# Reordering the first third of a cross-attention and MoE kernel on four engine queues

## The reference: what is computed

```python
def fake_quant(x, scale, zp):
    q = jnp.clip(jnp.round(x / s + z), 0, 255)
    return (q - z) * s
x = x + tanh(g_xattn) * (fake_quant(layernorm(x)) @ fake_quant(ctx))
# then, on layernorm(x): a router (softmax, 2 of 16 experts), the chosen experts and a shared one
z = silu(xt @ sw1 + sb1) * (xt @ sw2 + sb2) @ sw3 + sb3
x = x + tanh(g_ffn) * (y + z)
```

## Time and profile before

| | us |
|---|---|
| median of 3 runs (326.96 to 329.57) | 327.06 |
| the profiled execution's own time | 326.59 |
| its span, first to last instruction | 324.7 |
| PE busy | 299.0 |
| DVE busy | 186.0 |
| ACT busy | 104.7 |
| POOL busy | 25.7 |

### The profile page before, as it was taken

One profiled execution on the slowest core, in us unless ns is written; L12 is line 12 of the kernel. 1 busy time (PEld: TensorE's weight loads), 2 busy tenths in 40 slices (PEclk: granted clock), 3 DMA queues, 4 the chain that ended last, 5 costly groups with the idle time before them and its releaser, 6 DMA issues.

```text
span 324.7 us, 4586 instructions
## 1 busy us (share of the span) xinstructions
PE 299.0 (92%) x1892; PEld 151.5 (47%) x1892; DVE 186.0 (57%) x330; ACT 104.7 (32%) x113; POOL 25.7 (8%) x33
## 2 busy tenths in 40 slices
PE   0369879989999999999999999999999999999995
PEld 0234379964444444644444444444444344444442
DVE  2876897785698863585362565378674542110111
ACT  2888266868682450110343301313111000000000
POOL 2100120110000310000000011110121100000000
PEclk9999999999999999999999999999999999999999
DMA  7999044239960455000697600000000011300111
GB/s 285 415 314 290 1 131 131 63 96 230 308 215 0 91 105 129 2 2 0 182 342 256 219 40 2 0 0 0 2 0 0 4 67 67 129 28 36 67 65 65
DMA packets 34163, 35.55 MB, mean 109 GB/s; under 512 B 16068, under 2 KB 28380, under 8 KB 34012
## 3 DMA queue, kind: packets, MB, share of 16 engines
q1 hardware_dynamic: 34128, 35.23, 34.6%
...
HBM read 27.88 MB, written 4.20 MB: 99 GB/s over the span
## 4 chain that ended last, share of the span: by engine, by line
PE 80%; DVE 8%; SPq 7%; ACT 1%; DMA 1%; issue 1%; POOL 1%; DVEq 0%
PE PS L1312 26%; PE PS L1155 19%; PE PS L1369 19%; PE PS L1190 6%; PE PS L1102 6%; SPq L256 4%; DVE stats L662 2%; DVE areaW L716 2%; PE PS L1109 1%; DMA sbr<-in_L_ffn_sb_dram 1%; SPq L248 1%; DVE X L733 1%; PE PS L1171 1%; DVE wrow L742 1%; PE PS L1197 1%
## 5 line engine op out<-in xcount | busy, mean ns | idle before, releaser
L1155 PE MATMUL PS<-areaT,areaW 128*128 128x512 f16 x288 | 62.6, 379 | 1.4 <-DVE SA L747 1.4
L1155 PEld LDWEIGHTS PS<-areaT,areaW 128*128 128x128 f16 x288 | 28.0, 98 | 34.8 <-DVE SA L747 1.6
L1312 PE MATMUL PS<-areaT,area 128*128 128x512 f16 x192 | 41.6, 379 | 0.0
L1312 PE MATMUL PS<-areaT,areaW 128*128 128x512 f16 x192 | 41.6, 379 | 0.0
L896 DVE SCALAR_TENSOR_TENSOR X<-PS,cf,X 128x512 f32<-128x512 f32 x16 | 12.0, 751 | 47.6 <-PE PS L1369 47.1
L1102 PE MATMUL PS<-area,areaQ 128*128 128x512 f16 x128 | 30.5, 389 | 0.9 <-DVE area L699 0.5
L1312 PEld LDWEIGHTS PS<-areaT,area 128*128 128x128 f16 x192 | 18.8, 98 | 22.7
L1312 PEld LDWEIGHTS PS<-areaT,areaW 128*128 128x128 f16 x192 | 18.8, 98 | 22.7
L662 DVE BATCH_NORM_STATS2 stats<-X 128x6 f32<-128x512 f32 x32 | 20.5, 682 | 4.4 <-DMA X<-in_x_dram 4.2
L1369 PE MATMUL PS<-SW,areaH 128*128 128x512 f16 x96 | 22.0, 379 | 0.0
L1369 PE MATMUL PS<-areaW,QI 128*128 128x512 f16 x96 | 22.0, 379 | 0.0
...
## 6 DMA issues: line engine op xcount, KB each, us to landing
...
```

The costliest lines, as they stand in the source:

```text
L1155: last = mm(PS[:, SU_BANK[half * SC + c] + w, lo:hi], SW[:, wp, 2 * c + w, k, :], XT[:, xp, k, tk], start=(k == 0 and n == 0), stop=(k == ...
L1312: last = mm(PS[:, EU_BANK[u] + w, :], W12S[j][:, wp, k, cs], XT[:, xp, k, b * S:(b + 1) * S], start=(k == 0 and n == 0), stop=(k == KC - 1 ...
```

## The change

It touches order alone, on SP, ACT, DVE and PE, with one more small root on POOL. No matmul is added or taken away.

- **SP** interleaves the loads: tile 0, chunk 0, tile 1, chunks 1 to 4, tile 2, chunks 5 and 6, tile 3, chunk 7. The two bias loads into `sbr` stand ahead of the four weight chunks instead of behind them.
- **POOL** takes the roots of tiles 2 and 3 one by one, so that the counts on `coef1` become 1 to 6 instead of 1 to 5.
- **ACT** quantizes chunk 0 first and chunks 2 to 5 before tile 2; it copies all four turned tiles itself (before, DVE copied tiles 2 and 3); `ln_rows` writes the f16 rows first and the f32 rows second, for all eight tiles.
- **DVE** follows that order, loses two copies, gains one set of `coefs`, and makes `C1` after the last `ctx` chunk. Behind the first `at_done` it does `attend(0)`, `bn(0)` and `coefs(0)` before `attend(1)`; `row_terms`, `shared_biases` and `lo_chunk 0` come after that and ahead of `bn(1)`.
- **PE** does all chunks for tiles 0 and 1, ends both, then tile 2, then tile 3; the transposes of the second layernorm of tile 0 stand in the middle of tile 3.

The core of the diff:

```diff
@@ block.sync
+            load_tile(0)
+            load_ctx0(0)
+            load_tile(1)
+            for k in range(1, 5):
+                load_ctx0(k)
+            load_tile(2)
+            load_ctx0(5)
+            load_ctx0(6)
+            load_tile(3)
+            load_ctx0(7)
+            sp.dma_start(sbr[0:SC, :], sb1.rearrange("(c p) -> c p", p=P)).then_inc(sbr_in, 16)
+            sp.dma_start(sbr[SC:2 * SC, :], sb2.rearrange("(c p) -> c p", p=P)).then_inc(sbr_in, 16)
@@ block.gpsimd
-            rstd(2, 2, TB)
+            rstd(2, 1, 3)
+            rstd(3, 1, TB)
@@ block.scalar
             act.wait_ge(tanh_rdy, 2)
+            quant_ctx(0, 0)
             quant_x(0)
-            quant_ctx(0, 0)
+            quant_ctx(0, 1)
             quant_x(1)
             evac_q1(0)
-            quant_ctx(0, 1)
+            quant_ctx(0, 2)
             evac_q1(1)
+            for k in range(3, 6):
+                quant_ctx(0, k)
             quant_x(2)
-            quant_ctx(0, 2)
+            quant_ctx(0, 6)
+            quant_ctx(0, 7)
             quant_x(3)
-            for k in range(3, KC):
-                quant_ctx(0, k)
+            evac_q1(2)
+            evac_q1(3)
             for c in range(4):
                 hi_chunk("sw", c)
@@ block.vector
+            clamp_ctx(0, 4)
+            clamp_ctx(0, 5)
+            coefs(3, 1, cf[:, 3:4], None, sc6[:, 1:2])
+            clamp_x(2)
+            clamp_ctx(0, 6)
+            clamp_ctx(0, 7)
...
-            evac_q1(2)
...
-            evac_q1(3)
...
+            attend(0)
+            bn(0)
             link(v.tensor_scalar(cf[:, 9:10], sc6[:, 3:4], -1.0, HALF, ALU.mult, ALU.add))
             link(v.tensor_scalar(cf[:, 7:8], cf[:, 4:5], cf[:, 9:10], None, ALU.mult))
             link(v.tensor_scalar(cf[:, 6:7], cf[:, 7:8], cf[:, 8:9], float(D), ALU.mult, ALU.mult))
+            coefs(0, 1, None, XS, None)
+            attend(1)
             row_terms(0)
             shared_biases()
-            clamp_ctx(0, 7)
-            attend(0)
-            bn(0)
-            attend(1)
-            coefs(0, 1, None, XS, None)
+            lo_chunk("sw", 0)
             bn(1)
-            lo_chunk("sw", 0)
             ln2_lo(0)
+            lo_chunk("sw", 1)
+            lo_chunk("sw", 2)
             coefs(1, 1, None, XS, None)
+            lo_chunk("sw", 3)
             attend(2)
@@ block.tensor
+            for k in range(3, KC):
+                pe.wait_ge(q2_rdy, k + 1)
+                products(0, k)
+                products(1, k)
+                if k == 6:
+                    transpose_q1(2)
+            pe.wait_ge(c1_rdy, 1)
+            pe.wait_ge(s2_rdy, 1)
+            column_sums(0)
+            column_sums(1)
             transpose_q1(3)
             pe.wait_ge(q1_rdy, 3)
-            for k in range(3):
+            for k in range(KC):
                 products(2, k)
...
+            column_sums(2)
             pe.wait_ge(r1_rdy, 1)
             pe.wait_ge(sbT_rdy, 2)
-            for k in range(KC):
+            for k in range(4):
+                products(TB - 1, k)
+            transpose_tokens(0)
+            for k in range(4, KC):
                 products(TB - 1, k)
             column_sums(TB - 1)
-            transpose_tokens(0)
```

More of the change, by code:

```diff
@@ L486, in ln_rows @@
                 act.wait_ge(coef2, i + 1)
-                if i >= 2:
-                    act.wait_ge(ln_lo, i - 1)
-                nc.scalar.activation(rows[:, i % 2, :], X[:, i, :], ACT.Identity, bias=lnB[:, i:i + 1],
-                                     scale=lnA[:, i:i + 1]).then_inc(ln_xs, 1)
                 if i in (TB, TB + 1):
@@ L496, in ln_rows @@
                                      scale=lnA[:, i:i + 1]).then_inc(ln_hi, 1)
+                if i >= 2:
+                    act.wait_ge(ln_lo, i - 1)
+                nc.scalar.activation(rows[:, i % 2, :], X[:, i, :], ACT.Identity, bias=lnB[:, i:i + 1],
+                                     scale=lnA[:, i:i + 1]).then_inc(ln_xs, 1)
             def evac_q1(i):
@@ L1209, in _ @@
                 products(0, k)
[L1210 to L1213 removed]
             pe.wait_ge(q2_rdy, 3)
             products(0, 2)
[L1216 removed]
+            pe.wait_ge(q1_rdy, 2)
+            for k in range(3):
+                products(1, k)
+            for k in range(3, KC):
+                pe.wait_ge(q2_rdy, k + 1)
+                products(0, k)
+                products(1, k)
+                if k == 6:
[4 more added lines that the diff above has]
+            column_sums(1)
             transpose_q1(3)
             pe.wait_ge(q1_rdy, 3)
[L1219 removed]
+            for k in range(KC):
                 products(2, k)
[L1221 to L1225 removed]
+                if k == 3:
                     pe.wait_ge(q1_rdy, TB)
                     bias_columns()
[L1228 removed]
                     row_sums(0)
[L1230 to L1233 removed]
+            column_sums(2)
             pe.wait_ge(r1_rdy, 1)
             pe.wait_ge(sbT_rdy, 2)
[L1236 removed]
+            for k in range(4):
+                products(TB - 1, k)
+            transpose_tokens(0)
+            for k in range(4, KC):
                 products(TB - 1, k)
             column_sums(TB - 1)
[L1239 removed]
             for i in range(TB):
```

53 lines of the change are left out of this document (13 added, 40 removed).

## The result

The changed kernel takes **323.69 us** (median of 4 runs, 323.25 to 324.01), the kernel before 327.32 beside it (4 runs, 326.96 to 329.57): a ratio of 0.988, 95% interval 0.985 to 0.991. The medians are 3.6 us apart, and the ratio, which is not taken from the medians, comes to 4.0 us (327.32 x 0.0122); 2.0 were forecast. The time lies inside the range, near its low end. The profiled execution took 323.71 us, 321.9 of them in the span, so 1.8 lie outside it.

A forecast was written before the change was run, and what follows sets the result against it. PE's list was taken to set the end, so only its idle time could be gained: 2.2 us up to `first_blocks(0)` minus 0.2 before `shared_up` made 2.0, and 327.06 - 2.0 = 325.1 us, range 323.4 to 327.4.

The forecast's parts named there:

- walk through the front: From the loads to `first_blocks(0)`: queue times added from row prices, first sums at 27.3 and `first_blocks(0)` at 41.0, 2.2 us gained.
- root of tile 0: On POOL, between `bn(0)` and `coefs(0)`: priced at 0.55 us; at 1.46 the low half would come 0.9 later, 326.0.
- wait inside tile 3 for `ln2_lo(0)`: On PE in tile 3's products: one new wait of about 1.0 us for DVE's low half, replacing three older waits.
- wait for `ln2_lo(1)`: On PE between `first_blocks(0)` and `shared_up`: a new wait of 0.7 us for DVE, net 0.2 lost in that part.
- Sum: Whole kernel: 2.2 - 0.2 = 2.0 us gained, taken from the median of before, 327.06, to give 325.1.
- the hole: PE before `first_blocks(0)`, 39.30 to 43.60 in the old order: busy 1.24 of 4.30 us, with waits of 1.07, 0.87, 1.16.
- The clock rival: PE between 19 and 27 us, thinned by the new order, falls to 1.2 GHz: loss of 1, 328.1 us; chance 0.09.
- I carry a shift at 70.20 to the end in full: From `shared_up` to the end: order on PE and prices unchanged, so any gain there reaches the end whole.
- beside light DVE work: POOL's roots in the old profile: 0.55 us there, against 1.46 beside `lo_chunk` and `ln2_lo`, which read two SBUF tensors.
- eaten by DVE: DVE's front without slack: tile 2 late (1.3) or root long (0.9), 326.0 to 326.4, both 327.3; chance 0.20.
- doesn't do what it says: First sums early, but `first_blocks(0)` unmoved, low half late by 3 us; within 0.5 of before, counted in the 0.20 eaten case.
- more than forecast: DVE early in the front, so the waits of 1.0 at the low half and 0.7 at `ln2_lo(1)` go: 323.4; chance 0.09.

The follow-up runs named there:

- filled_hole: The kernel before with ten useless matmuls added in PE's waits around the transposes of tile 0's rows; 326.20 us, ratio 0.995 to the kernel before.
- after_again: The changed kernel, unchanged, timed and profiled once more beside the kernel before; 323.30 us, ratio 0.988.
- three_tiles: The changed kernel with PE's list of before, products of tiles 0 to 2 together, then tile 3; 335.56 us, ratio 1.025 to the kernel before.
- loads_alone: The kernel before with only SP's new order of loads; 330.51 us, ratio 1.010 to the kernel before.
- gate_sooner: rows_sooner with DVE's `su_gate(0)` moved up between `bn(6)` and `bn(7)`; 325.33 us, ratio 0.993 to the kernel before.
- rows_sooner: The changed kernel with ACT's `ln_rows(0)` between the second and third `hi_chunk` and DVE's first two `ln2_lo` moved up; 322.12 us, ratio 0.983 to the kernel before.

## Why the prediction missed the size

Its walk through the front came out almost row by row:

| step | forecast | measured |
|---|---|---|
| tile 2 lands | 14.5 | 14.59 |
| first sums | 27.3 | 27.20 |
| first `attend` can start | 28.3 | 28.35 |
| copies of q end on ACT | 30.5 | 30.5 |
| root of tile 0 | 0.55 | 0.55 |
| wait inside tile 3 for `ln2_lo(0)` | 1.0 | 0.99 |
| `first_blocks(0)` | 41.0 | 41.14 |
| wait for `ln2_lo(1)` | 0.7 | 0.50 |
| `shared_up`, wait ahead of it | 68.2, 1.4 | 68.00, 1.46 |

Part of this agreement is luck. The first sums start between 26.59 and 27.70 in the six profiles of kernels that are alike up to there, so any one date could have been half a microsecond off; the intervals behind the sums are what repeats, and there the walk has 13.7 us to `first_blocks(0)` where the trace has 13.94. So the mechanism of the front was right, and what failed is the **Sum**: "327.06 - 2.0 = 325.1". It took a shift from one profiled execution and set it against a median, as if all executions had the front of that one. They have not: 54 of 60 lose time to the 1.2 GHz level, 1.6 us on average over all 60, and the first profile of before, with a granted clock of 1.000, was one of the few that don't. The one fall that was profiled in this kernel begins in the hole, and filling the hole ends the falls in 7 of 7 runs. By closing the hole the change takes that loss away too. The term for it was missing, put at nothing without a reason. It is worth about 1.5 (filled_hole 1.45, the table 1.6).

The sign of this was in view. The clock rival asked whether the *new* order would fall to 1.2 GHz, and answered "no run here shows a fall after the start" from a single execution; it never asked whether the *old* one, with PE busy 1.24 of 4.30 us, falls in others. Of its three runs one stood at 329.57, and the profiled one 0.5 below their median; both were read as scatter. The rival itself fell: with two tiles a chunk and waits of 1.17 and 1.05 between 19 and 27 us the products stayed 0.22 apart, and the clock was 0.998 or more in all 10 runs.

The other 0.5 us is the 2.5 at equal clock against 2.0. With these two terms the sum is 2.0 + 1.6 + 0.5 = 4.1, which is the distance of the means (327.79 and 323.66 for the first runs) and near the 4.0 of after_again; the 3.6 between the first medians is the lowest of these readings. The profiled pair, both at full clock, is 2.9 apart, and there the excess of 0.9 can be placed: 0.2 because `shared_up` came at 68.00 and not 68.2; minus 0.1 between there and 173; and some 0.7 at the end, 0.4 of it in the pause ahead of the last stage and 0.3 in the tail. **"I carry a shift at 70.20 to the end in full"** was thus nearly right here. The pause scatters: from the start of the last matmul ahead of it to the start of the next it was 0.69 to 2.22 us over all profiles, with no order by kernel, so its 0.4 is luck of one pair. The tail's 0.3 repeats: it is 3.23 us in the nine profiles with DVE's and ACT's new lists, three_tiles among them, and 3.56 to 3.58 in the four with the old ones, loads_alone among them, so it goes with neither SP's list nor PE's alone. Its cause stays open: the last landing comes 2.0 us behind the end of DVE's last addition in both, and the difference lies behind that landing. Front and tail together, 2.2 + 0.3, are the 2.5 at equal clock within its scatter. And the rule has a condition that was never stated: gate_sooner brought `shared_up` 0.50 forward and lost 3.2, since DVE's order behind it had changed.

One reading of the rows was wrong without harm. The root that took 0.55 did not run "beside light DVE work": `attend(1)`, a long instruction, was under way (36.22 to 37.49). It reads one tensor from PSUM and only one from SBUF, so the row supports the price of 0.55 more than the text says.

The rivals "eaten by DVE" and "doesn't do what it says" fell with the table above; "more than forecast" has the time about right (323.4) and the reason wrong, since neither the wait at the low half nor the one for `ln2_lo(1)` went. That the time lies inside the range is luck too: the range reached down to 323.4 for a case that didn't happen. rows_sooner is what that rival described, 1.2 to 1.6 us with both of them gone, and it needed two lists to be rewritten, ACT's too.
